# Attention and feed-forward kernel: the copy of a transposed tile ahead of each step's minimum, and three smaller reorderings

## The reference

```python
q = layer_norm(x, g1, b1)
qh, kh, vh = heads(q @ wq + bq), heads(ctx @ wk + bk), heads(ctx @ wv + bv)
scores = einsum('bqhd,bkhd->bhqk', qh, kh) * hd ** -0.5      # masked to k <= q
o = merge(einsum('bhqk,bkhd->bqhd', softmax(scores), vh))
x = x + o @ wo + bo
out = x + gelu(layer_norm(x, g2, b2) @ w1 + b1) @ w2 + b2
```

## Time and profile before

| | |
|---|---|
| median of 3 runs | 2937.24 us (2937.08 to 2942.78) |
| profiled execution | 2934.94 us, span 2933.2 us |
| granted TensorE clock, mean | 0.985 |
| TensorE matmul busy | 2782.0 us, 95% of the span |
| TensorE weight loads busy | 2521.7 us, 86% |
| VectorE busy | 2030.9 us, 69% |
| ScalarE busy | 1657.2 us, 56% |
| GpSimd busy | 355.9 us, 12% |

### The profile page before, as it was taken

How to read it: one execution, slowest core, us unless ns; L and a number is a source line. 1 busy time by engine, 2 the same in 40 slices (tenths; PEclk the granted TensorE clock), 3 DMA queues, 4 the chain that set the end, 5 groups by cost and what they waited for, 6 DMA issues and landing times. The chain is left out here.

```text
span 2933.2 us, 65737 instructions
## 1 busy us (share of the span) xinstructions
PE 2782.0 (95%) x22056; PEld 2521.7 (86%) x22056; DVE 2030.9 (69%) x4884; ACT 1657.2 (56%) x4014; POOL 355.9 (12%) x364
## 2 busy tenths in 40 slices
PE   6999999999999999999984999999999999999999
PEld 4788777887778877788764999999999899999999
DVE  4777676766777667776657877787787766665566
ACT  3666666666666666566645456556555544444444
POOL 1211222112221122221210000000000000000000
PEclk9999999999999999999997999999999999999999
DMA  6667666676666666666634334434435344333342
GB/s 144 105 121 114 107 113 119 114 114 109 113 122 114 111 109 117 122 110 111 101 66 161 141 148 186 170 124 171 186 138 206 123 158 152 141 149 114 152 157 94
DMA packets 152506, 383.03 MB, mean 131 GB/s; under 512 B 12928, under 2 KB 17024, under 8 KB 144256
## 3 DMA queue, kind: packets, MB, share of 16 engines
q1 hardware_dynamic: 152448, 382.28, 53.6%
HBM read 172.51 MB, written 109.05 MB: 96 GB/s over the span
## 5 line engine op out<-in xcount | busy, mean ns | idle before, releaser
L726 ACT ACTIVATE sm<-sm,mins 128x128 f32<-128x128 f32 (+3 forms) x1024 | 571.6, 559 | 531.3 <-DVE mins L589 527.8
L589 DVE CUSTOM_DVE_ANT_0 sm<-bank_s,mask 128x128 f32<-128x128 f32 (+3 forms) x1024 | 479.5, 487 | 413.5 <-PE bank_s L441 404.4
L453 PE MATMUL bank_t<-ident,sm 128*128 128x128 f32 x2560 | 417.1, 277 | 47.0 <-DVE pT L536 32.9
L453 PEld LDWEIGHTS bank_t<-ident,sm 128*128 128x128 f32 x2560 | 303.1, 141 | 137.8 <-issue 45.6
L441 PE MATMUL bank_s<-stack 96*128 96x128 f32 (+3 forms) x1024 | 354.5, 387 | 7.0 <-DMA stack<-st_lo 7.0
L536 DVE COPY pT<-bank_t 128x384 f32<-128x384 f32 (+1 forms) x576 | 326.5, 567 | 0.5 <-PE bank_t L453 0.5
L1110 PE MATMUL bank_x<-b_hi,w_hi 128*128 128x256 f32 x1024 | 295.8, 289 | 23.6 <-DVE g L1311 9.6
L1110 PE MATMUL bank_x<-w_hi,a_hi 128*128 128x256 f32 x1024 | 291.7, 285 | 4.5 <-DVE a_lo L1230 4.5
L1112 PE MATMUL bank_x<-b_hi,w_lo 128*128 128x256 f32 x1024 | 291.6, 285 | 0.0
L1111 PE MATMUL bank_x<-b_lo,w_hi 128*128 128x256 f32 x1024 | 291.6, 285 | 0.0
L1111 PE MATMUL bank_x<-w_lo,a_hi 128*128 128x256 f32 x1024 | 291.3, 284 | 0.0
(11 more groups left out here) (178 smaller groups left out, 7411.7 us busy)
## 6 DMA issues: line engine op xcount, KB each, us to landing
stack<-st_hi SPq DMA_DIRECT2D x256, 256.0 KB, 6.1
stack<-st_lo SPq DMA_DIRECT2D x128, 256.0 KB, 7.4
xr<-x_scratch SPq DMA_DIRECT2D x32, 1024.0 KB, 6.0
b_scratch<-b_hi SPq DMA_DIRECT2D x16, 1792.0 KB, 9.9
b_scratch<-b_lo SPq DMA_DIRECT2D x16, 1792.0 KB, 13.9
b_hi<-b_scratch SPq DMA_DIRECT2D x16, 1792.0 KB, 7.4
b_lo<-b_scratch SPq DMA_DIRECT2D x16, 1792.0 KB, 11.2
xt<-in_x SPq DMA_DIRECT2D x64, 256.0 KB, 2.8
```

The costliest lines, as they stand in the source:

```text
L453: mm = pe.transpose(bank_t[n % 2][:, P * c:P * c + P], sm[:, n % SLOTS_S, P * c:P * c + P], ident[:])
L589: op = V.tensor_tensor_reduce(sm[:, n % SLOTS_S, off:off + w], bank_s[n % BANKS_S][:, off:off + w], mask[:, 512 - w:512], 1.0, 0.0, ALU.ad ...
L726: op = A.activation(row, row, ACT.Exp, bias=mins[:, g % 2, c:c + 1], scale=-1.0, accum_out=sums[:, g % 2, c:c + 1])
```

## The change

Four edits:

1. VectorE does `move_tile` first in a step, ahead of `mask_and_max` and `x_low`.
2. ScalarE takes two more tiles of group 2: tiles 3, 5, 7, 9, 11 in place of 5, 9, 11. The other groups keep 5, 9, 11.
3. In a step in which both a V job and an X job end, which is step (2,9) alone, ScalarE does `v_copy` ahead of `x_high`. V1b has 9, 9 and 6 matmuls in steps 7, 8, 9 in place of 8, 8, 8.
4. In stage B VectorE does `add(c, 0, "C22")` ahead of `normalise` 2 and 3.

```diff
-ACT_MOVES = (5, 9, 11)
-def act_moves(k):
-    return k in ACT_MOVES
+ACT_MOVES = [(5, 9, 11), (5, 9, 11), (3, 5, 7, 9, 11), (5, 9, 11)]
+def act_moves(n):
+    g, k = divmod(n, 12)
+    return k in ACT_MOVES[g % 4]
...
-        [... ("X0", {7: 4}), ("V1b", {7: 8, 8: 8, 9: 8}),
+        [... ("X0", {7: 4}), ("V1b", {7: 9, 8: 9, 9: 6}),
...
                 for n in range(len(it.steps) + it.tail):
                     g, k = divmod(n, TG)
+                    if (n > LAG and not it.tail or n <= LAG and not it.first) and not act_moves(n - LAG - 1):
+                        move_tile(dve, V.tensor_copy, it, n - LAG - 1)
                     if not it.tail:
                         mask_and_max(it, n)
                     for job, jg in it.ended(n):
                         if job[0] == "X":
                             x_low(it, job, jg, it.b + 1)
-                    if (n > LAG and not it.tail or n <= LAG and not it.first) and not act_moves((n - LAG - 1) % TG):
-                        move_tile(dve, V.tensor_copy, it, n - LAG - 1)
...
                 for n in range(len(it.steps)):
                     g, k = divmod(n, TG)
+                    x_ended = any(job[0] == "X" for job, _ in it.ended(n))
+                    for job, jg in it.ended(n):
+                        if job[0] == "V" and x_ended:
+                            v_copy(it, job, jg)
                     for job, jg in it.ended(n):
                         if job[0] == "X":
                             x_high(it, job, jg)
...
-                        if job[0] == "V":
+                        if job[0] == "V" and not x_ended:
                             v_copy(it, job, jg)
...
                 a_low(c, 0, 0)
+                add(c, 0, "C22")
                 if norm:
                     normalise(c + 1, 2)
                     normalise(c + 1, 3)
-                add(c, 0, "C22")
```

More of the change, by code:

```diff
@@ L765, in body @@
                         exponential(it, n)
-                    if (n > LAG and not it.tail or n <= LAG and not it.first) and act_moves((n - LAG - 1) % TG):
+                    if (n > LAG and not it.tail or n <= LAG and not it.first) and act_moves(n - LAG - 1):
                         move_tile(act, A.copy, it, n - LAG - 1)
```

## The result

| | before | after |
|---|---|---|
| median | 2938.62 us (4 runs, 2937.08 to 2942.78) | 2891.89 us (4 runs, 2889.73 to 2895.74) |
| profiled execution, span | 2934.94, 2933.2 us | 2895.74, 2894.0 us |
| granted TensorE clock, mean | 0.985 | 0.984 |

The ratio is 0.984, 95% interval 0.9823 to 0.9857: faster by 1.6%, 46.7 us by the medians, where 48.0 were forecast. The traces differ by 39.2 us only: the profiled execution before (2934.94 us, taken apart from these four) lies 3.7 us under their median, and the one after is the slowest of its four, 3.9 us over theirs.

The account below looks back on a forecast made before the run. TensorE, busy 95% of the span, was taken as the bound, with only its waits winnable. 24.8 + 8.3 + 5.7 - 1.5 + 1.5 + 9.2 = 48.0 us off 2937.24 gave 2889.2 us; range 2877 to 2902.

Parts of the forecast that it names:

- End of group 2: Stage A, 15 batches: TensorE's waits for V's copy and tile 6 go, less 0.55 us for tile 7; 24.8 us won.
- The clock: Stage A: the stretches at granted clock 0.50 behind the two waits go in six batches; 8.3 us won, bounds 0 and 9.7.
- The rival that the drops stay without the waits: Stage A: transposes alone keep the clock falling; 39.7 us won, 2897.5 us; no own chance, held within the forecast's 0.58.
- Group 3: Stage A, 15 batches: tile 3's wait goes, ScalarE's for tile 5 grows; 0.38 us a batch, 5.7 us won, bounds 0 and 20.
- Group 0: Stage A: the later minimum of step 7 delays the O0 product by 0.1 us a batch; 1.5 us lost, bounds 0 and 3.
- The last batch: End of stage A: no dense work in group 3, TensorE waits for VectorE's and ScalarE's tiles; 1.5 us won, between 0 and 3.
- Stage B: The wait for VectorE's addition goes: 14 rounds by 0.66 us, 9.2 us won, round 0 given 0; bounds 6.6 and 10.
- A smaller sign: Stage A waits: ScalarE's tile copies become TensorE's releasers, with shorter waits, in steps (2,10), (3,0) and (3,10).
- The slower rival: Stage A: later minimum adds 0.15 us for each of 34 tiles a batch; 82 us less the 48, 2971 us; chance 0.06.

## Why the prediction was right, point by point

- **End of group 2: right in place, order and size.** Steps (2,7) to (3,0) took 13.13 us without a lower clock and take 11.49: 1.64 us a batch, forecast 1.65. Both waits go, Q0's wait for X3's low half stays small (in the timeline after, 2.09 us from X3 to Q0 where 1.95 were put), and ScalarE's tile 7 costs 0.47 (forecast 0.55). Each of the two edits alone shortens these steps, by 0.90 and by 1.21 us; with both, and tile 7 back on VectorE, they take 11.01 us, 2.12 less than before (2.2 put): the sum.
- **Edit 2 was priced rightly as a loss** for tile 7 and as nothing for tile 3; both were run.
- **The clock: right for batches 2 to 14.** The lower clock is gone from every one of them, 8.3 us. The rival that the drops stay without the waits is out here: from V1b's end to Q0 there are still some 4 us of transposes, scores and PV products, and the clock is 1.00. The Trainium skill, TensorE: Matmul & The Clock Gate (PE-mode transpose), says that transposes do not count as busy in the way matmuls do. By that this stretch could have brought drops still; it brought none in 13 batches, and the measurement decides for this mixture. Whether transposes by themselves would hold the clock isn't shown, as scores and PV products stand between them. With either one of the two waits gone, batches 1 to 14 show no drop. Yet before both waits stood in each of these 14 batches, and six had one. Here are the waits of batch 9 before, and the stretch behind them at 1.00, to compare with the rows of batch 8 in the earlier trace rows:

```profile
944.90:948.30 3.40, 1.77 (x13) 1.21 (x11) 1.59 (x5) 2.50 (x7) 2.41 (x4) 1.00 0.40 96
948.40:951.70 3.30, 2.84 (x18) 2.54 (x19) 2.63 (x9) 1.80 (x6) 3.14 (x4) 1.00 0.98 338
```

So the two waits were needed in these traces and weren't enough. What else decides isn't shown; each kernel that lost a wait also has another batch length, and the two weren't tested apart. That all 8.3 us came back is what the prediction said, with its reason shown in part.
- **Group 3: size right, reason half right, and in part luck.** 0.32 us a batch, forecast 0.38; the exponentials run back to back as put. Step (3,8) gives 0.75 us and (3,10) takes 0.30 back for ScalarE, which would leave 0.45; the last 0.13 goes in step (3,11), to the landing of K0's stack copy, which the prediction did not name. Its slack of some 0.35 us happened to lie near the 0.38 put for ScalarE. The upper bound of 20 us for this term was out of reach.
- **Group 0:** (0,8) -0.09, (0,10) +0.19, net +0.09 us a batch, forecast +0.1, by the chain that was named.
- **The last batch: wrong in sign.** Forecast 1.5 us won with what follows, measured 6.8 us lost in the profiled executions. The steps themselves have no new wait of VectorE, and a new one for ScalarE (1.82 us, for tile 7, which edit 2 moved); and the loss stands beside 10 us at the lower clock, which the execution before did not have there. I had given the clock a term for the batches and none for the end of stage A, where little work covers the waits. What brings the lower clock there stays open. The length of ScalarE's wait isn't what decides: with edit 3 alone the wait in step (3,2) is 1.59 us, as before (1.58), and the last batch takes 89.3 us with 13.7 us of it at the lower clock. Edit 1 alone (1.96 us there) has 86.8 us and 6.8 at the lower clock, and the changed kernel without edit 2, with the same 1.96 us, 85.45 us and 3.4. Edit 4 alone has 85.5 us and none. Each of these is one execution.
- **Stage B:** 0.65 us a round, forecast 0.66. Round 0 won 1.2 us more (62.56 to 61.35 us), which I had put at nothing; it begins at a lower clock in both traces. It can't be put down to edit 4: over the kernels with the same stage B as the changed one round 0 takes 60.3 to 62.4 us (alone, edit 4 gave 9.9 us in the whole stage).
- **A smaller sign failed.** The prediction put ScalarE's tile among the releasers in step (2,10) too; the 20 waits in ten batches are those of (3,0) and (3,10) alone.
- **The slower rival** (the later minimum on the path) is out: the one place in which it showed is step (0,10), 0.19 us a batch.

The sum by profile is 15 x (1.64 + 0.32 - 0.09) + 8.3 + 10.3 - 6.8 = 39.9 us, against 39.2 between the two traces. (Batches 0 to 14 measured 35.3 in place of the 36.4 in this sum; batches 0 and 1, which have other work and clock, hold the rest.) The medians give 46.7. What lies between was not settled. The four executions after had a mean granted clock of 0.984 (the profiled one, the slowest), 0.987, 0.989 and 0.986, and the stretches at the lower clock at the end of stage A differ from trace to trace; they are the likeliest place, which is only argued. By the traces the forecast of 48.0 is 8.8 us too high, and the last batch is 8.3 of it; that the medians come within 1.3 us of it is in part luck.

## What to carry to other kernels

In an in-order engine, put the operation whose input comes first and whose output frees a buffer ahead of the one that waits for later work; the price is the delay of the later one, and it is worth looking up which single chain has no slack for it. Add up each won wait only as far as the next thing that is due, and look for that among the DMAs too: a copy that takes 8.7 us to land behind five others can be the next bound without a single row in the waits of before. To find it, compare each copy's landing with the instruction that needs it: here the slack was 0.35 us. Where a stage ends with little work, give the clock a range of its own there; the traces of this case differ by 10 us and more at the lower clock in the last batch.

## What the hardware showed that I had not expected

- In batches 1 to 14 the lower clock came only when the two waits (0.98 and 1.20 us of idle) stood together. With 0.98 or with 0.82 us alone it never came there. With both it came in every second batch, in batches 2 to 12 in one trace and 4 to 14 in the other, and cost 1.4 us each time.
- In the last batch before, two waits of 1.58 and 1.55 us, with TensorE busy 1.65 us in 3.40, brought no lower clock; with edit 3 alone, a wait of 1.59 us in the same step stood with 10.2 us of it.
- Six stack copies of 256 KB, issued within 5.3 us, landed 1.8 to 2.0 us apart, so that the last took 8.7 us from issue to landing; copies of 64 KB in their place took 2.0 us at the median. Loads of 512 KB in all, issued 1.2 us behind the last, put off its landing by 0.1 us.
